# Side work of the tensor engine in pairs every second quarter, and the distance squares of one batch element dealt out anew

## The chip, the cores and the metric

The kernel runs on one core of one Trainium2 chip. The metric is the device time of one execution in microseconds (us), the median of several. TensorE (PE in the rows; PEld is its loading of weights), VectorE (DVE), ScalarE (ACT), GpSimd (POOL) and SyncE (SP, which issues the DMAs) each run their own list of instructions in order, and wait for each other through semaphores.

## What is computed

The input x is 8 x 1024 x 256 (batch elements, tokens, channels), fp32. Four residual blocks follow one another, each on a layer norm of x:

```python
x = x + attn_a(_layernorm(x))   # scores from distances between 3-d positions of the tokens, causal
x = x + ffn(_layernorm(x))      # mixes a token with the one before it; gate * (relu(k)**2 @ W_v)
x = x + attn_b(_layernorm(x))   # 16 heads of 16 channels, softmax over keys, causal
x = x + ffn(_layernorm(x))

# attn_a, the part that the change touches
pos = x @ w3d.T + b3d
sq = jnp.sum((pos[:, :, None, :] - pos[:, None, :, :]) ** 2, axis=-1)
dist = jnp.sqrt(sq)
attn = softmax(-dist * scale, causal)      # one matrix for all heads
out = (attn @ V) @ wo.T + bo
```

## The kernel before

**Two kinds of work.** The third block (attn_b, "att3" in the code) is the steady beat of the kernel. Its work is cut into PIECES = 8 elements x 4 groups of 4 heads x 12 pieces, and each piece into 4 **quarters**, one a head. Quarter u issues on PE one matmul for the row maxima (L922, into max_bank), one for the transposed scores (L935, into exp_bank, for a piece LEAD = 14 pieces earlier), and where u % 4 == 3 also the four products with the values (L954, into o_bank). DVE takes the maxima (L989, L992), ACT the exponentials (L973). max_bank and exp_bank have two buffers each. An element takes 192 quarters; call that a **turn**. Batch element n's third block runs in turn n.

Everything else (layer norms, first block "att1", the two FFNs "ffn2" and "ffn4", the projections of the third block "proj3") is **side work**. It is done for later elements while the beat runs. On PE it consists of **jobs** (`tr` transposes L442, `keys` L741, `receptance` and `products` L755, `project` L825, `values3` L841, `values1` L615, `positions` L600, `attend` L633, and `output` and `maxima` of the beat itself, L1066 and L1032). A job owns one of three PSUM banks (`side0` to `side2`) from its first part until ACT or DVE has read it (for `project` that is ACT's L784, for `tr` L432, for `positions` L519).

**The order.** `place()` runs before anything is issued: it goes quarter by quarter, from BEGIN = -224, and gives each part of each job its quarter and each job its bank. At most one part a quarter, no part before its due time; a job starts only if a bank is free by the plan. `shift` is how late the plan is. `schedule()` then writes each engine's instructions: in a quarter first those of att3, then those of the side work. The other engines' side instructions stand at the quarters `at(k)`, which are the stage's own times plus that shift.

**The prologue** is u < 0: no beat yet, only side work for elements 0 and 1. It ends when PE issues the first L922 at u = 0. Element 0's chain is: set up weights, att1, ffn2, proj3, store the projected parts to DRAM and load them as stacks, then u = 0. Element 1's att1 and ffn2 lie between.

**Squares of distances** (functions `dve_squares`, `act_att1`, `pool_att1`, `dve_att1`). Each of att1's 12 pieces (512, 384, 256, 128, then 512 five times, 384, 256, 128 columns) needs three squares, one a coordinate. ACT makes the first two (L536), POOL adds them (L589), DVE adds the third (L468, which also keeps it above a tiny value), and ACT transforms the sum in three steps: logarithm (L550), exp of half of it (L553), exp (L560). POOL cuts the diagonal (L578). The third square is made on DVE for elements 0 and 1 (L508 and L511, `n < 2`), on ACT for the others. In `act_att1` the instructions alternate: square of piece p, transform of piece p - 1, square, transform, transform. sq holds two pieces.

**Rows of ones.** The stacks of keys need two rows of ones, 2 partitions x 4096 elements in each of three stacks. They are set by DVE in `dve_weights` (L1151), at quarters that fall into element 0's att1.

Of the kernel before, what the change touches and what calls it, by code (L numbers as in the profile page):

```python
# [35 lines left out]
KROWS = HD * len(K_SLOTS)  # L36
SROWS = KROWS + 2
MAX_BANKS, EXP_BANKS = 2, 2
STACKS = 3
# [105 lines left out]
def place():  # L145

    parts, delay = [], {}
    for start, s, n, h in STAGES:
        for key, first, count, step, after in stage_jobs(s, n, h):
            delay[key] = after  # L150
            parts += [(start + first + step * k, key, k, k == count - 1) for k in range(count)]
    parts.sort(key=lambda part: part[0])
    rows = [(4 * NP * (g + 1) + 1, ("maxima", g)) for g in range(GROUPS)]
    rows += [(OUTPUT_AT[h] + 4 * NP * g + 5, ("output", g, h)) for g in range(GROUPS) for h in range(2)]
    rows += [(at, ("setup", k)) for k, at in enumerate(SETUP_AT)]
    rows.sort()
    quarters, bank, emptied, late = {}, {}, {}, []
    free, before, shift, u = [BEGIN, BEGIN, BEGIN], BEGIN, 0, BEGIN
    while parts or rows:
        while rows and rows[0][0] <= u and min(free) <= u:  # L160
            key = rows.pop(0)[1]
            k = free.index(min(free))
            quarters[key], bank[key], emptied[key] = [u], k, u + 2
            free[k] = u + 2
        if parts:
            at, key, k, last = parts[0]
            regained = max(0, shift - max(0, at - before) // 4)
            if at + regained <= u and (k > 0 or min(free) <= u):
                parts.pop(0)
                before, shift = at, max(regained, u - at)  # L170
                late.append((at, shift))
                if k == 0:
                    bank[key] = free.index(min(free))
                    free[bank[key]] = NEVER
                    quarters[key] = []
                quarters[key].append(u)
                if last:
                    emptied[key] = free[bank[key]] = u + delay[key]
        u += 1
    return quarters, bank, emptied, late  # L180

# [21 lines left out]
def bass_hybrid(nc, x, wq, bq, wk, bk, wv, bv, wo, bo, w3d, b3d, wkqv, bkqv, w_r, w_k, w_v,  # L203
# [7 lines left out]
    with ExitStack() as ctx:  # L211
# [310 lines left out]
        def act_att1(at, n):  # L522
# [37 lines left out]
                    act.activation(p1[:, at:at + w], d, ACT.Exp, scale=-SCALE).then_inc(p1_exp, 1)  # L560

            for p in range(NP + 1):
                for k in range(3):
                    if p < NP and (k < 2 or n > 1):
                        yield at(PIECE_AT[p] + PIECE_TIME[p] * 2 * k // 6)
                        square(p, k)
                    if p > 0:
                        yield at(PIECE_AT[p] + PIECE_TIME[p] * (2 * k + 1) // 6)
                        transform(p - 1, k)
# [565 lines left out]
        def dve_weights():  # L1135
# [10 lines left out]
            yield SETUP_AT[7] + 6  # L1146
            dve.tensor_copy(wv3[:, :, :, :], raw_kqv[:, :, :, 2 * HD:3 * HD])
            dve.memset(rinv1[:, :], 0.0).then_inc(weights_ready, 1)
            for r in range(STACKS):
                yield SETUP_AT[7] + 12 + 8 * r  # L1150
                dve.memset(ks[r][KROWS:SROWS, :, :], 1.0).then_inc(rows_of_ones, 1)  # L1151

        def pe_setup():
            pe = nc.tensor

# [44 lines left out]
        def pool_setup():  # L1200
            pool = nc.gpsimd
            yield SETUP_AT[6] + 6
            pool.memset(vp[:, :, ONE:ONE + 1], 1.0).then_inc(consts_ready, 1)
            for k, v in enumerate(v3):
                yield SETUP_AT[7] + 4 * k
# [84 lines left out]
        def _(dve):  # L1290
# [1 line left out]
            dve.wait_ge(consts_ready, 5)  # L1292

            def stage(at, s, n, h):
                body = {"att1": [dve_att1(at, n)] + ([dve_squares(at, n)] if n < 2 else []), "proj3": [dve_proj3(at, n), dve_values3(at, n)]}.get(s, []) if h == 0 else []
                return [dve_statistics(at, s, n, h)] + ([dve_ffn(at, s, n, h)] if s in ("ffn2", "ffn4") else body)

            schedule([dve_setup(), dve_weights()], dve_att3, dve_maxima, dve_output, stage)
# [36 lines left out]
```

## Time and profile before

| | |
|---|---|
| median of 3 runs | 2104.41 us (2093.51 to 2106.41) |
| the profiled execution, device time | 2109.85 us |
| its span, first to last instruction | 2108.1 us |
| busy: PE, DVE, ACT, POOL | 1849.2, 1467.0, 1323.7, 728.2 us |
| the prologue (to the first L922) | 195.1 us |
| a turn in the middle of the kernel | 245.8 us |
| after the last exponentials | 42 us |

The profiled execution is 5.4 us above the median of the three runs. "Busy" of PE counts a matmul until its modelled end, so it says where PE is fed without a gap, and not how much of its peak it reaches.

### The profile page before, as it was taken

The page shows a single profiled execution, that of the slowest core. Times are in us where ns is not written, and L with a number is a line of the kernel's source. Part 1 is how long each engine was busy: PE and PEld are TensorE (multiplying, and loading weights), DVE is VectorE, ACT ScalarE, POOL GpSimd, SP SyncE. Part 2 cuts the span into 40 slices and gives each one's busy share as a digit, 9 for nine tenths or more (in the row PEclk, how much of TensorE's full clock was granted, in tenths as well). Part 3 has the DMA queues.
Part 4 walks back from the last instruction along what each step waited for, and adds up shares of the span by engine and source line. Part 5 has one row for each costly group of instructions (what it writes and reads, how often), then busy time and mean ns, then how long its engine had stood idle before and what let it go on. Part 6 is the DMA issues. An engine that isn't in the chain of part 4 may idle for free. (4 is left out here: it accounts for less than half of the span.)

```text
span 2108.1 us, 32379 instructions
## 1 busy us (share of the span) xinstructions
PE 1849.2 (88%) x9842; PEld 922.5 (44%) x9842; DVE 1467.0 (70%) x4288; ACT 1323.7 (63%) x2585; POOL 728.2 (35%) x879
## 2 busy tenths in 40 slices
PE   5677898889997999889998899979998899988986
PEld 4453443335543455434543355434544345322423
DVE  5576778767676677667786667766776677768642
ACT  3564355876569565776758665695657766455664
POOL 1342332234333253333443243333532334312313
PEclk8797899999998999999999899989999999989998
DMA  3006113111131112410132111311124101322000
GB/s 85 1 23 123 26 56 67 31 31 32 55 76 31 31 31 82 80 21 12 41 110 42 31 31 56 76 31 31 34 83 76 22 11 41 99 33 50 13 21 20
DMA packets 64346, 97.26 MB, mean 46 GB/s; under 512 B 15655, under 2 KB 58029, under 8 KB 58030
## 3 DMA queue, kind: packets, MB, share of 16 engines
q1 hardware_dynamic: 64174, 95.20, 20.2%
q8 instruction: 80, 1.31, 0.3%
q14 instruction: 92, 0.75, 0.1%
HBM read 61.09 MB, written 33.55 MB: 45 GB/s over the span
## 5 line engine op out<-in xcount | busy, mean ns | idle before, releaser
L973 ACT ACTIVATE pt<-exp_bank 128x512 f32<-128x512 f32 (+1 forms) x1216 | 698.9, 582 | 526.6 <-PE exp_bank L935 521.0
L989 DVE CUSTOM_DVE_ANT_0 max_bank<-max_bank,mask 128x128 f32<-128x128 f32 (+3 forms) x1024 | 501.8, 500 | 400.9 <-PE max_bank L922 386.4
L922 PE MATMUL max_bank<-ks,qs 96*128 96x512 bf16 (+3 forms) x1536 | 523.5, 346 | 85.9 <-DVE piece_max L992 44.9
L935 PE MATMUL exp_bank<-qs,ks 98*128 98x512 bf16 (+3 forms) x1536 | 515.4, 342 | 40.0 <-ACT pt L973 37.0
L992 DVE TENSOR_REDUCE piece_max<-max_bank 128x1 f32<-128x512 f32 x512 | 344.1, 686 | 94.4 <-PE max_bank L922 90.2
L954 PE MATMUL o_bank<-pt,v 128*17 128x512 f32 (+3 forms) x3072 | 334.1, 508 | 13.7 <-POOL pt L1011 11.0
L922 PEld LDWEIGHTS max_bank<-ks,qs 96*128 96x128 bf16 x1536 | 150.9, 99 | 399.5 <-DVE piece_max L989 140.9
L1011 POOL TENSOR_SCALAR_AFFINE_SELECT pt<-pt 128x512 f32<-128x512 f32 x256 | 171.5, 670 | 412.6 <-ACT pt L973 411.8
L935 PEld LDWEIGHTS exp_bank<-qs,ks 98*128 98x128 bf16 x1536 | 152.4, 100 | 236.0 <-ACT pt L973 118.5
L633 PE MATMUL side<-vp,p 128*128 128x260 f32 x576 | 171.4, 423 | 28.7 <-ACT p L560 21.0
L412 ACT ACTIVATE xh<-xs,shift,rstd 128x256 f32<-128x256 f32 x256 | 149.7, 596 | 47.8 <-POOL shift L401 47.8
L589 POOL TENSOR_TENSOR sq<-sq 128x512 f32<-128x512 f32 (+1 forms) x96 | 97.3, 1013 | 226.3 <-ACT sq L536 226.3
L536 ACT ACTIVATE sq<-pb,neg_pos 128x512 f32<-128x512 f32 (+3 forms) x264 | 167.0, 633 | 3.6 <-ACT p L560 0.4
L741 PE MATMUL side<-pb,wkT 128*128 128x512 f32 x240 | 139.3, 669 | 9.3 <-DVE pb L675 9.2
L989 DVE DVE_READ_ACCUMULATOR2_ANT piece_max<- 128x1 f32 x1024 | 144.5, 141 | 0.3
L633 PEld LDWEIGHTS side<-vp,p 128*128 128x128 f32 x576 | 111.2, 207 | 74.1 <-issue 31.1
L825 PE MATMUL side<-xt,wkq 128*128 128x512 f32 x256 | 136.8, 619 | 3.0 <-ACT xt L432 1.5
L755 PE MATMUL side<-wrT,pb 128*128 128x256 f32 x480 | 126.3, 387 | 0.0
L755 PE MATMUL side<-wvT,pb 128*128 128x256 f32 x480 | 125.7, 386 | 0.0
L1090 POOL TENSOR_TENSOR xs<-xs,on 128x256 f32<-128x256 f32 x64 | 49.3, 770 | 208.5 <-DVE on L1080 208.4
L664 POOL TENSOR_TENSOR xs<-xs,tm 128x512 f32<-128x512 f32 x64 | 98.3, 1541 | 66.2 <-DVE tm L692 66.2
L791 POOL TENSOR_TENSOR parts<-x,parts 128x512 bf16<-128x512 f32 x64 | 74.9, 1170 | 108.3 <-DVE parts L775 108.3
(119 smaller groups left out, 2348.4 us busy)
## 6 DMA issues: line engine op xcount, KB each, us to landing
parts_dram<-parts SPq DMA_DIRECT2D x64, 384.0 KB, 2.6
qs<-parts_dram SPq DMA_DIRECT2D x192, 128.0 KB, 7.2
ks<-parts_dram SPq DMA_DIRECT2D x32, 384.0 KB, 4.7
xs<-in_L_attn_a_x_dram SPq DMA_DIRECT2D x16, 512.0 KB, 4.2
ks<-parts_dram SPq DMA_DIRECT2D x32, 256.0 KB, 5.4
out_dram<-xs SPq DMA_DIRECT2D x16, 512.0 KB, 3.1
ks<-parts_dram SPq DMA_DIRECT2D x32, 128.0 KB, 5.8
qs<-neg_maxT SPq DMA_DIRECT2D x64, 8.0 KB, 1.9
```

The costliest lines, as they stand in the source:

```text
L412: act.activation(xh[:, t, :], src[:, TPH * h + t, :], ACT.Identity, bias=shift[:, r, t:t + 1], scale=rstd[:, r, t:t + 1]).then_inc(xh_read ...
L536: mm = act.activation(sq[:, p % 2, c, 0:w], pb[:, c, q0:q1], ACT.Square, bias=neg_pos[:, kt, c:c + 1])
L633: mm = pe.matmul(bank[:, 0:VC], p1[:, at:at + P], vp[:, kt, :], start=(kt == 0), stop=(kt == t))
L741: mm = pe.matmul(bank[:, :], wkT[:, c, P * j:P * (j + 1)], xk[:, c, :], start=(c == 0), stop=(c == NC - 1))
L755: mm = pe.matmul(bank[:, C * t:C * (t + 1)], lhs[:, c, P * (2 * j + t):P * (2 * j + t + 1)], rhs[:, c, :], start=(c == 0), stop=(c == NC - 1))
L922: pe.matmul(max_bank[u % MAX_BANKS][:, 0:k1 - k0], qs[r][0:KROWS, j, P * tile:P * (tile + 1)], ks[r][0:KROWS, j, k0:k1], start=True, stop= ...
L935: mm = pe.matmul(exp_bank[k % EXP_BANKS][:, (q1 - q0) * slot:(q1 - q0) * (slot + 1)], ks[r][:, j, P * kt:P * (kt + 1)], qs[r][:, j, q0:q1] ...
L954: mm = pe.matmul(o_bank[32 * j:32 * j + VW, q0 - HALF * h:q1 - HALF * h], v3[n % 2][:, kt, GH * (g % NG) + j, :], pt[:, (e - 1) % 2, j, 0: ...
L973: act.activation(pt[:, e % 2, j + 1 - heads:j + 1, 0:w], exp_bank[k % EXP_BANKS][:, 0:heads * w].rearrange("p (j n) -> p j n", j=heads), A ...
L989: dve.tensor_tensor_reduce(scores, scores, mask[:, HALF - w:HALF], 1.0, LOWEST, ALU.add, ALU.max, piece_max[:, j, m:m + 1]).then_inc(max_f ...
L992: dve.tensor_reduce(piece_max[:, j, m:m + 1], scores, AX.X, ALU.max).then_inc(max_free, 1)
L1011: pool.affine_select(out=block, in_=block, compare_op=ALU.is_ge, fill=0.0, base=0, pattern=[[0, GH], [1, P]], channel_multiplier=-1).then_ ...
```

## The change

1. `place()`: for u < 0 it is as before, one part a quarter. For u >= 0 parts are placed in odd quarters only, up to two of them, and a part may be taken one quarter ahead of its due time (first part of a job) or two quarters ahead (a later part). Bank rules stay.
2. `act_att1`, element 0: the two squares of piece p stand together ahead of the three transforms of piece p - 1.
3. `dve_squares` is used for element 0 alone; for element 1 the third square goes to ACT, as it did for elements 2 to 7.
4. The three settings of rows of ones go from `dve_weights` to `pool_setup`, ahead of POOL's other settings there, behind a wait for the second layer norm's shift.

```diff
-        if parts:
+
+        for _ in range(1 if u < 0 else 2 * (u % 2)):
+            if not parts:
+                break
             at, key, k, last = parts[0]
             regained = max(0, shift - max(0, at - before) // 4)
-            if at + regained <= u and (k > 0 or min(free) <= u):
-                parts.pop(0)
...
+            if at + regained > u + (u >= 0) * (1 if k == 0 else 2) or k == 0 and min(free) > u:
+                break
+            parts.pop(0)
...
             for p in range(NP + 1):
+                for k in range(2 if n == 0 and p < NP else 0):
+                    yield at(PIECE_AT[p] + k)
+                    square(p, k)
                 for k in range(3):
-                    if p < NP and (k < 2 or n > 1):
+                    if p < NP and n > 0:
                         yield at(PIECE_AT[p] + PIECE_TIME[p] * 2 * k // 6)
                         square(p, k)
...
-            for r in range(STACKS):
-                yield SETUP_AT[7] + 12 + 8 * r
-                dve.memset(ks[r][KROWS:SROWS, :, :], 1.0).then_inc(rows_of_ones, 1)
...
             yield SETUP_AT[6] + 6
+            pool.wait_ge(shift_ready, 2)
+            for r in range(STACKS):
+                pool.memset(ks[r][KROWS:SROWS, :, :], 1.0).then_inc(rows_of_ones, 1)
+            pool.wait_ge(rows_of_ones, STACKS)
             pool.memset(vp[:, :, ONE:ONE + 1], 1.0).then_inc(consts_ready, 1)
...
-                body = {"att1": [dve_att1(at, n)] + ([dve_squares(at, n)] if n < 2 else []), ...
+                body = {"att1": [dve_att1(at, n)] + ([dve_squares(at, n)] if n == 0 else []), ...
```

Lines of the changed kernel stand 4 lower from `place()` to `act_att1`'s loop and 7 lower behind it: L536 is L540, L550 is L554, L468 is L472, L922 is L929, L935 is L942, L954 is L961, L825 is L832, L841 is L848.

**Place 1, element 0's att1, DVE.** From the last settings of the transposed weights to the end of the second piece (384 columns). Before:

```order
L1133 COPY wvT<-side 128x256 x2
L1151 MEMSET ks 2x4096
L508 TENSOR_SCALAR sq<-pb,neg_pos 128x512
L511 TENSOR_TENSOR sq<-sq 128x512
L468 SCALAR_TENSOR_TENSOR sq<-sq 128x512
L508 TENSOR_SCALAR sq<-pb,neg_pos 128x384
L511 TENSOR_TENSOR sq<-sq 128x384
L1151 MEMSET ks 2x4096
L468 SCALAR_TENSOR_TENSOR sq<-sq 128x384
```

Now:

```order
L1140 COPY wvT<-side 128x256 x2
L512 TENSOR_SCALAR sq<-pb,neg_pos 128x512
L515 TENSOR_TENSOR sq<-sq 128x512
L472 SCALAR_TENSOR_TENSOR sq<-sq 128x512
L512 TENSOR_SCALAR sq<-pb,neg_pos 128x384
L515 TENSOR_TENSOR sq<-sq 128x384
L472 SCALAR_TENSOR_TENSOR sq<-sq 128x384
```

The settings of `ks` have left DVE's list; a third one stood in the same way ahead of the 128-column piece. On ACT in the same place, squares of the 384- and 256-column pieces and transforms of the pieces before them. Before:

```order
L536 ACTIVATE sq<-pb,neg_pos 128x384
L550 ACTIVATE sq<-sq 128x512
L536 ACTIVATE sq<-pb,neg_pos 128x384
L553 ACTIVATE sq<-sq 128x512
L560 ACTIVATE p<-sq 128x512
L536 ACTIVATE sq<-pb,neg_pos 128x256
L550 ACTIVATE sq<-sq 128x384
```

Now:

```order
L540 ACTIVATE sq<-pb,neg_pos 128x384 x2
L554 ACTIVATE sq<-sq 128x512
L557 ACTIVATE sq<-sq 128x512
L564 ACTIVATE p<-sq 128x512
L540 ACTIVATE sq<-pb,neg_pos 128x256 x2
L554 ACTIVATE sq<-sq 128x384
```

The second square of a piece no longer stands behind the logarithm of the piece before it.

**Place 2, element 1's att1, ACT**, among the steps of element 0's FFN gate (L713, L717, L720 before; L720, L724, L727 now). Before:

```order
L560 ACTIVATE p<-sq 128x512
L536 ACTIVATE sq<-pb,neg_pos 128x256
L550 ACTIVATE sq<-sq 128x384
L713 ACTIVATE xs<-side 128x512
L720 ACTIVATE xs<-xs 128x512
L536 ACTIVATE sq<-pb,neg_pos 128x256
L717 ACTIVATE xs<-xs 128x512
L553 ACTIVATE sq<-sq 128x384
L560 ACTIVATE p<-sq 128x384
L720 ACTIVATE xs<-xs 128x512
```

Now:

```order
L564 ACTIVATE p<-sq 128x512
L540 ACTIVATE sq<-pb,neg_pos 128x256
L554 ACTIVATE sq<-sq 128x384
L720 ACTIVATE xs<-side 128x512
L727 ACTIVATE xs<-xs 128x512
L540 ACTIVATE sq<-pb,neg_pos 128x256
L724 ACTIVATE xs<-xs 128x512
L557 ACTIVATE sq<-sq 128x384
L540 ACTIVATE sq<-pb,neg_pos 128x256
L564 ACTIVATE p<-sq 128x384
L727 ACTIVATE xs<-xs 128x512
```

One more square a piece stands ahead of the gate's last step.

**Place 3, the projections of a later element, PE, with buffer numbers.** Project job 2 of element 5 and the first part of job 3. Before:

```order
L825 MATMUL side1<-xt,wkq 128x512
L922 MATMUL max_bank1<-ks1,qs1 128x128
L935 MATMUL exp_bank0<-qs2,ks2 128x256
L954 MATMUL o_bank<-pt,v30 17x384 x4
L825 MATMUL side1<-xt,wkq 128x512
L922 MATMUL max_bank0<-ks1,qs1 128x256
L935 MATMUL exp_bank1<-qs2,ks2 128x128
L841 MATMUL side0<-wv3,xt 128x256 x2
L922 MATMUL max_bank1<-ks1,qs1 128x256
L935 MATMUL exp_bank1<-qs2,ks2 128x128
L825 MATMUL side2<-xt,wkq 128x512
```

Now:

```order
L832 MATMUL side2<-xt,wkq 128x512 x2
L929 MATMUL max_bank0<-ks1,qs1 128x128
L942 MATMUL exp_bank0<-qs2,ks2 128x256
L929 MATMUL max_bank1<-ks1,qs1 128x128
L942 MATMUL exp_bank0<-qs2,ks2 128x256
L961 MATMUL o_bank<-pt,v30 17x384 x4
L832 MATMUL side2<-xt,wkq 128x512
```

Job 2's two parts stand together, and job 3 follows in the same bank two quarters later, where before it had another bank. The plan's shift at the middle turns is 0 to 2 quarters, where before it was 0 to 4.

## Rows read from the trace of the kernel before

**Rows 1.** Stretches A:B: length; busy PE, PEld, DVE, ACT, POOL (count); granted clock, DMA, GB/s
```profile
0.00:195.10 195.10, 128.23 (x514) 94.58 (x514) 121.31 (x278) 105.86 (x205) 68.53 (x91) 0.85 0.19 46
394.70:633.50 238.80, 218.05 (x1228) 110.95 (x1224) 176.22 (x528) 162.79 (x325) 90.28 (x108) 1.00 0.22 50
...
1370.80:1616.60 245.80, 225.89 (x1228) 113.95 (x1224) 176.54 (x526) 164.91 (x328) 91.03 (x108) 0.96 0.21 48
```

**Rows 2.** The same for stretches of turn 4, and where its clock falls
```profile
1125.10:1180.20 55.10, 43.86 (x238) 17.01 (x235) 36.70 (x108) 49.31 (x102) 19.46 (x27) 0.91 0.18 30
...
1207.00:1338.50 131.50, 127.90 (x664) 67.49 (x663) 98.49 (x289) 80.62 (x154) 55.93 (x60) 0.97 0.17 47
...
1207.10:1213.80 6.70, 6.09 (x19) 1.74 (x18) 5.94 (x11) 3.74 (x7) 1.82 (x3) 0.50 0.00 0
```

**Rows 3.** DVE in order of time: start, length, line, instruction [idle before <-what ended it]
```profile
40.59 0.69 DVE L468 SCALAR_TENSOR_TENSOR sq<-sq 128x512 f32<-128x512 f32 x1
...
43.12 3.47 DVE L1151 MEMSET ks<- 2x4096 bf16 x1 [0.91 <-DVE sq L511]
46.62 0.56 DVE L468 SCALAR_TENSOR_TENSOR sq<-sq 128x384 f32<-128x384 f32 x1
...
54.94 0.28 DVE L468 SCALAR_TENSOR_TENSOR sq<-sq 128x128 f32<-128x128 f32 x1
```

**Rows 4.** POOL in order of time, the same stretch
```profile
23.15 0.55 POOL L1206 MEMSET v<- 128x128 f32 x2
37.73 1.26 POOL L589 TENSOR_TENSOR sq<-sq 128x512 f32<-128x512 f32 x1 [14.03 <-ACT sq L536]
42.53 1.00 POOL L589 TENSOR_TENSOR sq<-sq 128x384 f32<-128x384 f32 x1 [3.54 <-ACT sq L536]
...
50.30 0.46 POOL L589 TENSOR_TENSOR sq<-sq 128x128 f32<-128x128 f32 x1 [0.73 <-ACT sq L536]
```

**Rows 5.** POOL's settings of other tiles, from one line's view: durations in ns min/median/max
```profile
L1262 POOL MEMSET ident<- x1: 205/205/205, 0.8 to 0.8; 128x128 f32 x1
L1262 POOL MEMSET mask<- x1: 530/530/530, 1.1 to 1.1; 128x512 f32 x1
```

**Rows 6.** ACT in order of time: pieces of element 0, then the gate of its FFN
```profile
58.35 0.63 ACT L550 ACTIVATE sq<-sq 128x512 f32<-128x512 f32 x1 [0.79 <-DVE sq L468]
...
63.04 0.63 ACT L550 ACTIVATE sq<-sq 128x512 f32<-128x512 f32 x1 [1.42 <-DVE sq L468]
...
136.18 0.61 ACT L720 ACTIVATE xs<-xs 128x512 f32<-128x512 f32 x1
```

**Rows 7.** PE in order of time, prologue
```profile
57.88 3.80 PE L633 MATMUL side<-vp,p 128*128 128x260 f32 x8 [3.86 <-issue]
...
80.59 2.04 PE L741 MATMUL side<-pt,wkT 128*128 128x512 f32 x2 [7.27 <-issue]
```

**Rows 8.** Stretches of 20 us, element 1's att1 beside element 0's proj3
```profile
120.00:140.00 20.00, 19.64 (x88) 14.17 (x87) 11.47 (x25) 16.18 (x36) 8.08 (x11) 1.00 0.01 1
140.00:160.00 20.00, 10.86 (x38) 6.65 (x36) 19.56 (x38) 9.61 (x19) 10.44 (x10) 0.90 0.17 59
```

**Rows 9.** Groups: line, count | busy us, mean ns | idle (L536: 100 to 200 us)
```profile
L536 ACT ACTIVATE sq<-pb,neg_pos 128x512 f32<-128x512 f32 (+3 forms) x24 | 14.6, 608 | 0.8
L511 DVE TENSOR_TENSOR sq<-sq 128x512 f32<-128x512 f32 (+3 forms) x24 | 15.0, 623 | 0.8
L508 DVE TENSOR_SCALAR sq<-pb,neg_pos 128x512 f32<-128x512 f32 (+3 forms) x24 | 12.7, 528 | 0.1
```

**Rows 10.** Turn 4, PE and ACT in order of time: banks' matmuls, a reader, waits
```profile
1303.81 1.13 PE L841 MATMUL side<-wv,xt 128*128 128x256 f32 x4 [0.82 <-ACT xt L432]
...
1307.37 1.02 PE L825 MATMUL side<-xt,wkq 128*128 128x512 f32 x2
...
1309.15 0.68 ACT L784 ACTIVATE x<-side,cols 128x512 f32<-128x512 f32 x1
...
1335.59 0.63 PE L442 MATMUL side<-ident,xh 128*128 128x128 f32 x4 [0.59 <-ACT x L784]
```

More of the change, by code:

```diff
@@ L164, in place @@
             free[k] = u + 2
-        if parts:
+        for _ in range(1 if u < 0 else 2 * (u % 2)):
+            if not parts:
+                break
             at, key, k, last = parts[0]
             regained = max(0, shift - max(0, at - before) // 4)
-            if at + regained <= u and (k > 0 or min(free) <= u):
-                parts.pop(0)
[L170 to L178, printed above, removed]
+            if at + regained > u + (u >= 0) * (1 if k == 0 else 2) or k == 0 and min(free) > u:
+                break
+            parts.pop(0)
+            before, shift = at, max(regained, u - at)
+            late.append((at, shift))
+            if k == 0:
+                bank[key] = free.index(min(free))
+                free[bank[key]] = NEVER
+                quarters[key] = []
+            quarters[key].append(u)
+            if last:
+                emptied[key] = free[bank[key]] = u + delay[key]
         u += 1
@@ L1294, in stage @@
             def stage(at, s, n, h):
-                body = {"att1": [dve_att1(at, n)] + ([dve_squares(at, n)] if n < 2 else []), "proj3": [dve_proj3(at, n), dve_values3(at, n)]}.get(s, []) if h == 0 else []
+                body = {"att1": [dve_att1(at, n)] + ([dve_squares(at, n)] if n == 0 else []), "proj3": [dve_proj3(at, n), dve_values3(at, n)]}.get(s, []) if h == 0 else []
                 return [dve_statistics(at, s, n, h)] + ([dve_ffn(at, s, n, h)] if s in ("ffn2", "ffn4") else body)
```

## Prediction, made before the changed kernel ran

> **What bounds the kernel now.** I read the busy times of the page first (the table above): PE is busy for 88% of the span, DVE 70%, ACT 63%. A share over the whole span hides the stages, so the second view is that of stretches. It shows three parts. The prologue takes 195.1 us, with no engine busy for more than two thirds of it: a chain of waits. A turn takes 245.8 us in the middle of the kernel and 238.8 us once, early, with the same 1228 PE matmuls; the granted clock is 1.00 in the short one and 0.96 in the long ones [rows 1]. Third, within a turn the first 55 us have ACT busy for 49.3 (it bounds them), and the 131 us from the FFNs to the projections have PE busy for 127.9 [rows 2]. Where ACT bounds, it is idle for nothing a PE order could mend; where PE bounds, only 3.6 us a turn are PE idle time.
>
> So edit 1 (pairs) works in the turns, and edits 2 to 4 work in the prologue, where the plan's quarters are unchanged. Whatever the prologue loses, the end loses: the beat starts when element 0's stacks are loaded.
>
> **Edit 4, rows of ones off DVE.** Each takes 3.47 us on DVE [rows 3]. What counts is how late each makes the sum of the piece it stands ahead of. First piece: POOL's sum of two squares ends at 37.73 + 1.26 = 38.99 [rows 4], DVE adds the third at 40.59 [rows 3]: 1.6 us late. Second: 43.53 against 46.62, 3.1 us. Fourth: 50.76 against 54.94, 4.2 us, of which I leave 1.2 for four short instructions of DVE's own that stand between: 3.0. ACT's logarithm waits for each. Sum 7.7 us.
>
> On POOL, no setting of 4096 elements stands in the trace. 128 elements take 205 ns and 512 take 530 [rows 5], a slope of 0.85 ns an element: 3.6 us each, 10.7 for the three. They start when POOL is free of the second layer norm, 23.1, end near 34, and the small settings behind them [rows 4] near 34.6. POOL's next work is the sum at 37.73, idle for 14 us before it. So they cost nothing, with 3 us to spare; bounds are nothing and, at twice the slope, 21 us, which ends at 45 and makes the first sum 7 us late. I take the slope: it is the same operation on the same engine. The GPSIMD Engine Reference of the Trainium skill (introduction) calls GpSimd the wrong choice for ordinary elementwise arithmetic, the Vector engine being "roughly 2x faster". By that rule the settings would end at 45 and the saving would nearly be used up; DVE's 3.47 us for 4096 are 0.85 ns an element too, so for settings this trace does not agree with it.
>
> **Edit 2, squares ahead.** With a square between logarithm and transform, one 512-column piece follows the other in 63.04 - 58.35 = 4.7 us [rows 6]: logarithm, square, POOL's sum, DVE's sum, one behind the other. With both squares ahead, POOL and DVE work while ACT transforms the piece before, and ACT's own five instructions set the pace: 2 x 0.7 + 3 x 0.63 + 0.3 for their hand-overs = 3.6 us. But layer norm 2 of the first half waits for the first four pieces only (the attend job of PE at 57.88 [rows 7]), and there it gives some 0.5 us. The five later long pieces gain 1.1 us each; PE comes to their attends only behind the first keys job at 80.59 [rows 7], which waits for that layer norm and not for them. I take 0.5, with 0 and 6 as bounds. Edits 2 and 4: -8.
>
> **Edit 3, element 1's third square from DVE to ACT.** It takes half of 27.7 us, 13.9, from DVE and adds 12 x 0.61 = 7.3 us to ACT [rows 9]. From 120 to 140 us ACT is the fuller of the two (16.2 of 20, DVE 11.5) [rows 8]; four added squares (0.7 + 0.6 + 0.5 + 0.4 = 2.2 us) stand ahead of the gate's last step, which ends at 136.8 [rows 6], and through it POOL's sum into x and the layer norm of proj3: +2.2. From 140 to 160 DVE is full (19.6 of 20) [rows 8] and that layer norm's statistics stand in its queue behind the squares of three pieces, 3 x 1.15 = 3.5 us: -3.5. Later squares are in ACT's gaps or the like on both sides. Net -1; bounds -4 (ACT's gaps take all) and +7 (all of ACT's share is late).
>
> **Edit 1, pairs.** No matmul is added. Half of the odd quarters hold the value products, and half the pairs follow them; before, a quarter of the parts did, so the switches are as many. With two buffers for maxima and for scores, two quarters' beat (0.9 us) then two parts (1.7 us) leave DVE and ACT the same 2.6 us to give a buffer back. What moves are the waits for side banks and inputs. A reader takes its time: project's last matmul ends at 1308.39, the bank is free at 1309.83, 1.4 us [rows 10]. Now job 3 follows job 2 in one bank with 0.85 us of PE work between (place 3): 0.7 us of waiting. In the same way, counted from the order at 1.4 to 1.7 us a reader: job 1 0.4, the output job behind project 7 0.9, the third positions job 1.0, and the two first values jobs, now two quarters behind their transposes instead of three, 0.9 each. Sum 4.9 us a turn. What goes are such waits of before: 0.82 and 0.59 [rows 10], and six smaller of the kind and the first attend's in the same turn, 4.4 in all by my reading of PE's order of time. Net +0.5 a turn, +3 for the six full turns; bounds -2.5 and +4 a turn.
>
> **Sum.** -8 - 1 + 3 = -6 us on the profiled execution's 2109.85: 2103.9. That execution is 5.4 above the median of the runs shown, so on the median's scale 2098.
>
> **Rivals.**
> - *The turns lose their clock falls.* At 1207.10 the clock is at half (1.2 of 2.4 GHz) for 6.7 us, just as the FFNs begin [rows 2]; the turn without falls is 7.0 us shorter [rows 1]. The keys jobs now start a quarter earlier and closer together, so a fall could pass. For it: the same work did run a turn at 1.00. Against: PE's load in the stretch before does not change, and four turns repeat the fall. All four: 28 us less, 2070 on the median's scale.
> - *Side banks bind more than I count* (the other side: slower). Place: projections to positions, where DVE and PE are both near full, so a reader's 1.4 us is often longer. If all new waits come and none of the old goes: +4.9 x 6 = 29 instead of 3, 2124. It decides from 1.5 us a turn on, where it eats the prologue's 9. The clock may join in, from 1.00 to 0.5 in places. The page TensorE: Matmul & The Clock Gate of the Trainium skill ("A second HAM failure mode") says that small idle times between groups of matmuls make the clock oscillate, which speaks against pairs with bare quarters between; rows here show falls in the thin stretches alone.
> - *POOL at twice the slope:* +7, 2105.
> - *The prologue gives nothing:* element 1's squares on ACT are late by their full 7.3 instead of -1. -8 + 7 + 3: 2106 and, without edit 1's 3, 2103.
>
> **Chances.** Forecast 0.46, clock falls lost 0.18, banks bind 0.16, POOL 0.05, prologue for nothing 0.15. One per cent, about what a measurement of this kernel can tell from no change, is 21 us: below 2083 or above 2125. The first rival lies mostly below, with a tail of the forecast: faster 0.25. The second is over 2125 in its worst part, and with a clock fall more: slower 0.11. Range: 2072 takes in half of the first rival, 2120 the second up to 4 us a turn (2098 + 3.5 x 6 = 2119).
>
> **What would show it.** The first L922 starts near 186 instead of 195.1; element 0's attend job for the fourth tile starts near 50 instead of 57.88; POOL's settings end before 35. In element 1, statistics of proj3's second half end some 1 to 3 us earlier than the shift of the whole. Turns of 246 +/- 3 with falls at the same place say that pairs are neutral; turns near 239 at 1.00 are the first rival; idle time of PE ahead of side jobs over 8 us a turn is the second. Settings of 7 us on POOL are the third. If the prologue shrinks by 9 and the end does not, a turn has taken it back, and the view by turns says which.

## The result and the profile after

| | before | changed |
|---|---|---|
| median | 2105.41 us | 2214.32 us (2211.22 to 2225.35, 4 runs) |
| ratio, 95% interval | | 1.054 (1.0487 to 1.0594) |
| profiled execution, device time / span | 2109.85 / 2108.1 us | 2211.22 / 2209.5 us |
| first beat (u = 0) | 195.1 us | 193.2 us |
| turns 1 to 5, mean length | 244.4 us | 262.4 us |
| of that, without PE busy | 20.2 us | 34.8 us |

The changed kernel is 5.4% slower. The forecast was 2098 us and the range ended at 2120. A fourth execution of the kernel before took 2414.66 us; it moves that median from 2104.41 to 2105.41 us, and the ratio is that of fast executions alone.

The first view of the changed kernel is that of stretches, one a turn from u = 192 on (columns as in [rows 1]):

```profile
397.40:656.50 259.10, 223.85 (x1229) 111.95 (x1225) 171.97 (x525) 162.81 (x326) 87.78 (x108) 0.98 0.21 46
656.50:921.40 264.90, 230.90 (x1227) 115.20 (x1225) 172.86 (x527) 164.21 (x328) 88.19 (x108) 0.95 0.20 45
921.40:1182.60 261.20, 225.37 (x1229) 112.78 (x1225) 172.93 (x527) 163.87 (x328) 88.52 (x108) 0.97 0.21 45
```

The first of them answers to the turn of 238.8 us in [rows 1]. The matmuls are as many (1229) and the clock is nearly as high (0.98). Yet it takes 20 us more, and 14.5 us of these are PE idle time: 259.10 - 223.85 = 35.3 against 20.8. Over turns 1 to 5 the mean grows by 18.0 us, 14.6 of them idle, 3.4 busy at a lower clock. Five such turns are 90 us; turn 0, turn 6 and the tail add 4.5, 6.7 and 2.0, and the prologue takes 1.9 off. That is the 101.4 us between the two spans. Within a turn, 13.2 of the 18.0 us lie in quarters 73 to 166, the stretch in which PE was busy nearly all the time [rows 2]: 143.3 us in place of 130.1 on average, with 14.8 us of PE idle time in place of 3.3.

The second view is that of PE's waits over the whole run: what PE was about to do, whom it waited for, us in total, times, longest. Before:

```profile
PE max_bank L922 <- DVE piece_max L992: 44.9, 80, 1.4
PE side L442 <- ACT xh L412: 22.8, 7, 9.7
PE side L741 <- DVE pb L675: 9.2, 3, 3.6
```

and changed:

```profile
PE side L446 <- ACT xh L416: 61.5, 45, 9.7
PE max_bank L929 <- DVE piece_max L999: 47.4, 78, 1.7
PE side L748 <- DVE pb L682: 40.6, 29, 3.6
PE side L1039 <- DVE neg_max L1008: 13.7, 21, 1.0
PE side L622 <- ACT xt L436: 10.6, 8, 1.8
PE side L832 <- ACT x L791: 6.7, 7, 1.1
```

The two waits that grew most, by 70 us together, are not for a bank. They are for *inputs* of side jobs: xh, the normalised rows that `tr` transposes, and the mixed rows (in pb) that `keys` multiplies. Of the waits for xh some 21 us belong to the prologue in either kernel. From the first beat on they are, before and changed:

```profile
PE side L442 <- ACT xh L412: 1.8, 3, 1.3
PE side L446 <- ACT xh L416: 41.5, 41, 1.6
```

All of PE's waits from the first beat on, added up: ahead of side jobs 48.7 us before and 138.4 changed, ahead of the beat's own matmuls 133.7 and 136.8. So the idle time came almost wholly ahead of side jobs. Waits for the reader that gives a side bank back, the rival I had priced, went from 13 to 29 us (L832 <- L791 is 6.7 of them); xh and the mixed rows went from 11 to 82.

One such wait, turn 4, PE in order of time:

```profile
1254.43 0.38 PE L929 MATMUL max_bank<-ks,qs 96*128 96x512 bf16 x1
1254.65 0.33 PE L942 MATMUL exp_bank<-qs,ks 98*128 98x384 bf16 x1
1255.72 0.66 PE L446 MATMUL side<-ident,xh 128*128 128x128 f32 x4 [0.74 <-ACT xh L416]
```

and ACT beside it:

```profile
1254.69 0.49 ACT L980 ACTIVATE pt<-exp_bank 128x384 f32<-128x384 f32 x1 [1.06 <-PE exp_bank L942]
1255.08 0.59 ACT L416 ACTIVATE xh<-xs,shift,rstd 128x256 f32<-128x256 f32 x1
```

This xh stands in ACT's order in quarter 60, behind that quarter's place in the beat. PE issues the beats of quarters 60 and 61 within 0.4 us, because quarter 60 has no part any more, and stands before the transpose of quarter 61 while ACT has just come to the exponential ahead of the xh. So ACT waits for PE (1.06 us), and then PE for ACT (0.74 us). Before, the same transpose stood in quarter 62:

```profile
1195.55 1.04 PE L633 MATMUL side<-vp,p 128*128 128x260 f32 x4
...
1197.19 0.60 PE L442 MATMUL side<-ident,xh 128*128 128x128 f32 x4
```

A part of 1.04 us lay between the beats of quarters 60 and 61 (L922 at 1195.16 and 1196.42), then came the beat of quarter 62, and the xh was there.

### The profile page after: what moved, and what is told of

Same layout as the page of the kernel before. It is cut to its first block and busy times, and to the rows that moved or that the text cites. A ratio compares the mean times of both kernels' runs of the same rounds, so it can differ in the third digit from the quotient of the medians.

```text
span 2209.5 us, 32354 instructions
## 1 busy us (share of the span) xinstructions
PE 1862.3 (84%) x9842; PEld 924.9 (42%) x9842; DVE 1433.9 (65%) x4261; ACT 1320.0 (60%) x2597; POOL 722.1 (33%) x882
## 5 line engine op out<-in xcount | busy, mean ns | idle before, releaser
L980 ACT ACTIVATE pt<-exp_bank 128x512 f32<-128x512 f32 (+1 forms) x1216 | 685.8, 579 | 591.1 <-PE exp_bank L942 588.8
L996 DVE CUSTOM_DVE_ANT_0 max_bank<-max_bank,mask 128x128 f32<-128x128 f32 (+3 forms) x1024 | 495.4, 503 | 459.9 <-PE max_bank L929 449.4
L929 PE MATMUL max_bank<-ks,qs 96*128 96x512 bf16 (+3 forms) x1536 | 513.7, 343 | 89.1 <-DVE piece_max L999 47.4
L942 PE MATMUL exp_bank<-qs,ks 98*128 98x512 bf16 (+3 forms) x1536 | 502.6, 338 | 39.3 <-ACT pt L980 36.6
L961 PE MATMUL o_bank<-pt,v 128*17 128x512 f32 (+3 forms) x3072 | 338.1, 513 | 14.6 <-POOL pt L1018 11.8
L929 PEld LDWEIGHTS max_bank<-ks,qs 96*128 96x128 bf16 x1536 | 151.7, 99 | 375.3 <-DVE piece_max L996 134.4
L942 PEld LDWEIGHTS exp_bank<-qs,ks 98*128 98x128 bf16 x1536 | 152.1, 100 | 189.8 <-ACT pt L980 89.8
L540 ACT ACTIVATE sq<-pb,neg_pos 128x512 f32<-128x512 f32 (+3 forms) x276 | 171.6, 626 | 3.6 <-ACT p L564 0.4
L640 PE MATMUL side<-vp,p 128*128 128x260 f32 x576 | 157.0, 409 | 15.3 <-ACT p L564 10.4
L748 PE MATMUL side<-pb,wkT 128*128 128x512 f32 x240 | 130.4, 671 | 40.6 <-DVE pb L682 40.6
L446 PE MATMUL side<-ident,xh 128*128 128x128 f32 x512 | 84.1, 291 | 69.6 <-ACT xh L416 61.5
L832 PE MATMUL side<-xt,wkq 128*128 128x512 f32 x256 | 134.8, 626 | 8.9 <-ACT x L791 6.7
L762 PE MATMUL side<-wrT,pb 128*128 128x256 f32 x480 | 116.6, 386 | 0.0
L762 PE MATMUL side<-wvT,pb 128*128 128x256 f32 x480 | 116.6, 386 | 0.0
L446 PEld LDWEIGHTS side<-ident,xh 128*128 128x128 f32 x512 | 58.1, 145 | 135.2 <-ACT xh L416 89.2
```

What stands on the lines that cost most here:

```text
L540: mm = act.activation(sq[:, p % 2, c, 0:w], pb[:, c, q0:q1], ACT.Square, bias=neg_pos[:, kt, c:c + 1])
L640: mm = pe.matmul(bank[:, 0:VC], p1[:, at:at + P], vp[:, kt, :], start=(kt == 0), stop=(kt == t))
L748: mm = pe.matmul(bank[:, :], wkT[:, c, P * j:P * (j + 1)], xk[:, c, :], start=(c == 0), stop=(c == NC - 1))
L762: mm = pe.matmul(bank[:, C * t:C * (t + 1)], lhs[:, c, P * (2 * j + t):P * (2 * j + t + 1)], rhs[:, c, :], start=(c == 0), stop=(c == NC - 1))
L929: pe.matmul(max_bank[u % MAX_BANKS][:, 0:k1 - k0], qs[r][0:KROWS, j, P * tile:P * (tile + 1)], ks[r][0:KROWS, j, k0:k1], start=True, stop= ...
L942: mm = pe.matmul(exp_bank[k % EXP_BANKS][:, (q1 - q0) * slot:(q1 - q0) * (slot + 1)], ks[r][:, j, P * kt:P * (kt + 1)], qs[r][:, j, q0:q1] ...
```

## The experiments

Two theories stood at the start. **Inputs late**: a part that is moved ahead meets an input whose producer stayed at its place, behind its own quarter's beat. **Bunched**: two parts in one go hold back the beat. Neither is the whole. The differences in us below are the measured ratio less 1, times about 2100.

### Which edit

> The kernel before with edit 1 alone: the rule that places the side jobs' parts, nothing else. All theories that put the loss into the side parts expect nearly the whole difference: the turns of the changed kernel are 14 to 20 us longer each, its prologue is 1.9 us shorter, so 2211 to 2220 us here. A theory that the memsets on POOL or the third squares on ACT cost the time expects 2105 us.

2219.37 us, ratio 1.0578 (1.0527 to 1.0630). Edit 1 carries the whole loss: 121 us beside 114, with intervals that overlap.

> Edits 2, 3 and 4 without edit 1: the changed kernel with the old rule for the side jobs' parts. If edit 1 carries the whole loss, this gains what the prologue shows in the changed kernel's trace, 1.9 us, and about 1 us at element 1: 2100 to 2104 us. DVE's copies between 24 and 33.4 us should again take 2.2 to 3.6 us in place of 0.43, beside POOL's memsets.

2102.91 us, ratio 1.0004 (0.9971 to 1.0037). No difference can be measured. First beat at 194.2 us, so most of the 9 us that the prediction gave to the prologue are missing, and the loss in the turns is another matter. A first beat is read from one execution and has a spread of its own: in the eight kernels whose instructions up to it are those of the kernel before, it lies between 194.4 and 198.4 us, 196.7 on average. With edits 2 to 4 as in the changed kernel it lies at 191.8, 193.2 and 194.2.

### Pairs and lead apart

Pairs, nothing earlier:

```diff
 PARTS_AT, BANK, EMPTIED_AT, LATE = place()      # as before
+MOVED = ("setup", "maxima", "output")
+PARTS_AT = {key: [u + (u >= 0 and u % 2 == 0 and key[0] not in MOVED) for u in at] for key, at in PARTS_AT.items()}
```

> Pairs without looking ahead: the side jobs are planned as before, and then every part of an even quarter moves into the odd one behind it. 2 parts stand between two beats of the attention as in the changed kernel, but no part stands earlier than before. Theory 'inputs late' (TensorE stands before parts whose input comes from engines that are still behind their quarter's beat): no input is needed earlier, so about 2105 us, at most 2115. Theory 'bunched' (two parts together hold back the beat, whose rings of banks then run dry): about the same loss as the changed kernel, 2190 us or more.

2132.15 us, ratio 1.0168 (1.0118 to 1.0217): +35 us.

Lead, no pairs:

```diff
-        for _ in range(1 if u < 0 else 2 * (u % 2)):
+        for _ in range(1):
```

> Looking ahead without pairs: at most one part in a quarter, in every quarter, but by the changed rule a part may stand 1 (a job's first) or 2 quarters ahead of its time. The parts stand on average 1.17 quarters earlier than before, in the changed kernel 1.18. Theory 'inputs late': the same margin of 1 quarter, 2.2 us, is taken from every input, so a loss like the changed kernel's, 2170 to 2215 us. Theory 'bunched': about 2105 us.

2138.03 us, ratio 1.0193 (1.0133 to 1.0253): +41 us.

Both theories missed both numbers. Each half costs something, and 35 + 41 = 76 falls short of the 114 to 121 us of the two together. The waits say that the two costs are of different kinds. Pairs without lead:

```profile
PE max_bank L924 <- DVE piece_max L994: 64.5, 97, 1.4
PE side L444 <- ACT xh L414: 22.8, 7, 9.7
PE o_bank L956 <- POOL pt L1013: 21.0, 23, 1.5
PE side L743 <- DVE pb L677: 9.2, 3, 3.6
```

Lead without pairs:

```profile
PE max_bank L926 <- DVE piece_max L996: 41.1, 74, 2.0
PE side L745 <- DVE pb L679: 31.9, 30, 3.6
PE side L446 <- ACT xh L416: 29.9, 14, 9.7
PE o_bank L958 <- POOL pt L1015: 3.8, 9, 1.2
```

Pairs leave the inputs as before (22.8 and 9.2) and lengthen the waits of the beat itself (maxima from 44.9 to 64.5). Lead leaves the beat and lengthens the waits for inputs (9.2 to 31.9, 22.8 to 29.9). The sums from the first beat on, in us:

| kernel | PE's waits ahead of side jobs | ahead of the beat |
|---|---|---|
| before | 48.7 | 133.7 |
| pairs in odd quarters | 37.8 | 164.4 |
| lead, single parts | 85.9 | 117.9 |
| changed | 138.4 | 136.8 |

In the changed kernel the price that pairs have alone, waits of the beat, has gone again, and all the loss stands ahead of side jobs.

The run with lead and single parts changes one thing more. The side instructions of the other engines are written by the plan's shift, and a plan with lead is less late. Worked out from the plans, they stand one or two quarters earlier in 30% of the quarters there and in 22% in the changed kernel, 0.35 and 0.34 quarters on average; in the runs that move parts after the plan is made they stand where they stood. No run has the lead of this one with those instructions held in place, so its 41 us are not shown to be those of the parts alone. The next run is free of this.

### How much lead

```diff
-            if at + regained > u + (u >= 0) * (1 if k == 0 else 2) or k == 0 and min(free) > u:
+            if at + regained > u + (u >= 0) * 1 or k == 0 and min(free) > u:
```

> The kernel before with pairs, but the lead cut to 1 quarter for every part: 415 of 844 parts of the attention's quarters stand 1 quarter earlier than before, 429 where they stood (in the changed kernel 375 stand 1, 249 stand 2 and 40 stand 3 quarters earlier). If the cost of a pair grows with the lead, this lies between the pairs without lead (+34 us) and the changed kernel (+115 us): by the mean leads (-0.5, 0.49 and 1.18 quarters) at +80 us, 2180 us. If only parts that stand 2 or more quarters early reach their inputs too soon, it lies near the pairs without lead: 2130 to 2145 us.

2161.78 us, ratio 1.0272 (1.0250 to 1.0293): +57 us. It lies between the two forecasts, so the loss begins with the first quarter of lead and grows behind it. Here the other engines' side instructions stand as in the kernel before. Against the pairs without lead, the same 415 parts stand two quarters earlier, and the readers of their banks with them: 22 us more, and the waits ahead of side jobs go from 37.8 to 87.5 us.

### The inputs earlier

> The changed kernel with the inputs that TensorE waited for most moved 2 quarters ahead in their engines' orders: the layer norms (statistics on DVE, deviation on POOL, xh on ACT) and the token mixing of the feed-forward (xk and xr on DVE). Everything else as in the changed kernel. Theory 'inputs late': the waits of the changed kernel for xh (61.5 us in all, 22.8 before) and for the mixing (40.6 us, 9.2 before) fall back to about the old values, so 60 to 70 us are regained: about 2145 us, with the waits for other inputs and for the maxima left. Theory 'bunched' (pairs themselves, whatever stands in them): nothing is regained, 2200 us or more.

2182.60 us, ratio 1.0367 (1.0338 to 1.0396). About 35 us come back, not 60 to 70. The named waits went as forecast: xh is at its old value, and mixing is down from 40.6 to 6.4, 74 us less together. But in the profiled execution the beat's own waits grew by 26 us, from 136.8 to 162.5, and PE was busy for 21 us more at a lower clock (0.939 beside 0.948):

```profile
PE max_bank L936 <- DVE piece_max L1006: 62.0, 103, 1.7
PE exp_bank L949 <- ACT pt L987: 41.8, 92, 1.3
PE side L452 <- ACT xh L422: 21.3, 5, 10.0
```

> The changed kernel with every clocked instruction of ACT, DVE, POOL and SP that belongs to side work moved 1 quarter ahead (the takers of the side banks stay where they are). The parts stand 1.18 quarters ahead on average, so this gives back most of the lead to the inputs, but not to the second parts of pairs, which stand 2 ahead. Theory 'inputs late': more than half of the 115 us regained, 2120 to 2155 us, not less than the 2132 us of the kernel with pairs and no lead by more than 10. Theory 'bunched': 2200 us or more.

2175.55 us, ratio 1.0345 (1.0305 to 1.0385): 40 us come back, less than "more than half".

> Pairs with a lead of at most 1 quarter (+55 us when run before), and every clocked instruction of side work on ACT, DVE, POOL and SP 1 quarter ahead. Against their inputs the parts stand on average 0.51 quarters later than before, like the pairs without lead (0.49). Theory 'the lead costs by the inputs, the pair by the beat': the two are the same, +34 us within 10: 2125 to 2145 us, with waits for xh near 22 us. If the side work that is now ahead of the beats on ACT and DVE costs in its own right: +50 us or more.

2152.06 us, ratio 1.0269 (1.0222 to 1.0316). The same as without the earlier inputs (1.0272), where 1.016 was forecast. xh fell from 38.1 to 22.6 us, as said, and the wait for POOL's part of the beat rose from 11.6 to 28.0. The next run shows that price alone.

> The kernel with the rows of ones set on ACT and edits 2 and 3, and in addition every clocked instruction of side work on ACT, DVE, POOL and SP 1 quarter ahead in its engine's order, with the parts of TensorE where they always stood. If the old places of the inputs already left TensorE waiting (37 us of waits for side inputs in the kernel before lie mostly in the prologue), up to 5 us are gained on the 2081 to 2094 us of the kernel without it; if the beats of DVE and ACT are now held back by work that is not yet due, the waits for the maxima grow and it is slower by 5 to 15 us. Forecast: within 1% of the kernel without it.

2136.27 us, ratio 1.0183 (1.0128 to 1.0238), where the kernel without it has 0.9928 (below): 2.6% slower, 54 us. The forecast of "within 1%" is wrong. To have the inputs earlier has a price of its own:

```profile
PE max_bank L925 <- DVE piece_max L995: 50.7, 83, 1.4
PE exp_bank L938 <- ACT pt L976: 43.7, 93, 1.0
PE o_bank L957 <- POOL pt L1014: 29.2, 34, 1.6
PE side L442 <- ACT xh L412: 22.5, 6, 10.1
```

Waits for POOL's part of the beat, 11.4 us in the kernel without it, are 29.2 here, and those for the exponentials rose from 35.9 to 43.7; all waits of the beat together from 131.6 to 162.6. Each move by one quarter also changes which side instruction stands behind which instruction of the beat on three engines. That this is the reason is argued, not shown. So the runs that moved inputs measure a gain less this price and can't size "inputs late" alone; that it exists is shown by the waits, not by their times. In the changed kernel itself, where side instructions moved too, the beat's waits hardly grew (133.7 to 136.8), so nothing like this price shows there.

### Which quarter

In the even quarters instead, nothing earlier (`u % 2 == 1` in the diff of the pairs without lead):

> Pairs without looking ahead as in the run with +34 us, but in the even quarters: every part of an odd quarter moves into the even one behind it. The value products of the attention (4 matmuls, every fourth quarter, always an odd one) then no longer stand beside a pair. Theory 'pairs hold back the beat': +25 to +45 us again. Theory 'the pair collides with the value products': at most +10 us, 2098 to 2116 us.

2090.88 us, ratio 0.9976 (0.9946 to 1.0006). The same pairs cost nothing. "Bunched" falls, in the form in which I had put it. It is the place of the pair.

> Pairs without lead, but only in every fourth quarter, that of the value products: parts of quarters with remainder 2 by 4 move into the one with remainder 3, all others stay. Theory 'collision with the value products': these 227 moved parts carry nearly the whole loss of the pairs in odd quarters, +25 to +35 us, 2125 to 2135 us. Theory 'odd quarters as such (the exponentials run there)': half of it, +17 us, 2115 us.

2133.89 us, ratio 1.0135 (1.0090 to 1.0179): +28 us.

> The counterpart: parts of quarters with remainder 0 by 4 move into the one with remainder 1, behind which no value products stand. Theory 'collision': within 8 us of the kernel before, 2090 to 2106 us. Theory 'odd quarters as such': +17 us, 2115 us.

2115.40 us, ratio 1.0058 (1.0034 to 1.0082): +12 us. So 28 of the 35 to 40 us belong to the quarter with the value products (227 parts moved), 12 to the other odd one (188 parts moved). The forecasts were 25 to 35, and under 8 or 17. The mean time from one quarter's L922 to the next, in us, worked out from the starts of all of them in turns 1 to 6, shows what happens there:

| kernel | u % 4 = 0 | 1 | 2 | 3 | four quarters |
|---|---|---|---|---|---|
| before | 0.88 | 1.07 | 1.17 | 1.94 | 5.06 |
| pairs in odd quarters | 0.43 | 1.56 | 0.62 | 2.55 | 5.16 |
| pairs in even quarters | 1.40 | 0.58 | 1.67 | 1.37 | 5.02 |
| lead, single parts | 0.86 | 1.23 | 1.20 | 1.84 | 5.13 |
| changed | 0.38 | 2.00 | 0.58 | 2.45 | 5.41 |
| changed, pairs in even | 1.53 | 0.60 | 1.72 | 1.30 | 5.15 |

The quarter of the value products is the longest already. A pair there, without lead, makes it 2.55 us on average, and in turn 4's quarter 91 of that kernel it is 3.3 us from L922 to L922 (1248.59 to 1251.87). DVE and ACT have two quarters of beat in their buffers for that time and no more; then the next two beats follow within 0.4 us of each other, and PE waits for DVE. In the even quarters the long stretches of PE work are 1.4, 1.7 and 1.4 us.

> The changed kernel with its pairs in the even quarters, all else as in it. The planner then gives the parts a mean lead of 0.66 quarters in place of 1.18 (6 parts 3 quarters ahead, 111 two, 368 one, 304 none, 55 one behind). Theory 'an odd quarter is the wrong place for a pair, since every second one carries the value products': the 34 us of the pairs go, and what the lead costs beside single parts (40 us at a lead of 1.17) goes down with it, so 2105 to 2130 us. Theory 'pair and lead together cost, wherever the pair stands': by the lead alone (+55 us at 0.49, +115 us at 1.18) 2160 us or more.

2142.24 us, ratio 1.0175 (1.0125 to 1.0225): +37 us in place of +114. The place takes two thirds of the loss away, with the lead going from 1.18 to 0.66 quarters as part of it. It is 12 us above the forecast's upper end of 2130. Its waits of the beat add up to 137.2 us, as in the changed kernel; those ahead of side jobs fell from 138.4 to 81.4. So in the changed kernel the odd quarters, and the larger lead that goes with them, cost through the inputs and not through the beat. The waits:

```profile
PE max_bank L929 <- DVE piece_max L996: 52.0, 128, 1.3
PE max_bank L929 <- DVE piece_max L999: 47.5, 78, 1.8
PE side L446 <- ACT xh L416: 24.0, 8, 10.1
```

Why pair and lead together cost more than their sum is to be seen by the transposes. Of the 55 `tr` pairs of the beat's time (one for each half layer norm), so many have their first part one quarter behind the last xh, the others two or more:

| kernel | one behind | what stands in the quarter between the two | waits for xh |
|---|---|---|---|
| before | 0 | a part | 22.8 us, 7 times |
| pairs in odd, no lead | 0 | | 22.8 us, 7 times |
| lead, single parts | 43 | a part, mostly | 29.9 us, 14 times |
| pairs in odd, lead of 1 | 40 | nothing | 38.1 us, 39 times |
| changed | 46 | nothing | 61.5 us, 45 times |
| changed, pairs in even | 9 | | 24.0 us, 8 times |

(The counts are worked out from the plan, the waits read from the traces; some 21 us and 4 times of each are the prologue's.) The last xh mostly stands in an even quarter. With single parts that quarter still has its part, which gives ACT its time. With pairs in odd quarters it is bare, 0.4 us long, and PE arrives at once. The waits for xh and mixing together are 61.5 + 40.6 us in the changed kernel and 29.9 + 31.9 in the one with single parts and lead, 40 us more, beside the 38 us by which 114 exceeds 76. That fits, but it isn't proof: where the waits were taken away by earlier inputs, 74 us of them, only 35 came back. Why the changed kernel waits 23 us longer for xh than the pairs with a lead of 1, at nearly the same count, stays open.

### The prologue

Here the changed kernel's DVE, in order of time, from 24 us on:

```profile
24.00 2.23 DVE L1151 COPY wkq<-p 128x128 f32<-128x128 f32 x2
26.16 0.74 DVE L456 TENSOR_TENSOR vp<-side,bias_vp 128x259 f32<-128x259 f32 x2
26.82 3.01 DVE L1151 COPY wkq<-p 128x128 f32<-128x128 f32 x2
29.76 3.56 DVE L463 TENSOR_SCALAR neg_pos<-vp 128x12 f32<-128x12 f32 x1
29.82 3.49 DVE L1140 COPY wrT<-side 128x256 f32<-128x256 f32 x1
30.16 3.29 DVE L1151 COPY wkq<-p 128x128 f32<-128x128 f32 x2
```

and POOL's settings:

```profile
22.58 10.71 POOL L1208 MEMSET ks<- 2x4096 bf16 x3
```

Three settings, 3.57 us each on average, end near 26.1, 29.7 and 33.3. DVE's copies, 0.44 us for two of them before, end at 26.23, 29.83 and 33.45. A tensor_scalar on 12 elements a partition took 3.56 us, 0.17 before. Each was held until the setting beside it was over, and PE then waited, by its waits:

```profile
PE side L622 <- DVE wrT L1140: 4.2, 1, 4.2
```

The positions jobs began at 39.22 us in place of 31.75, 7.5 us later, and that is all that was to be saved (7.7).

> The kernel before with edits 2 and 3, and the three memsets of the rows of ones neither on DVE nor on POOL but on ACT, which has nothing to do from 2.1 to 13.0 us of the span. Theory 'POOL's memset holds DVE': with the memsets away from POOL DVE's copies between 24 and 34 us take 0.43 us again, the first element's pieces start 7 to 8 us earlier than before, and the prediction's gain of the prologue comes true in part: the first beat of the attention at 186 to 190 us in place of 195.1, the whole 4 to 8 us shorter than before, 2090 to 2094 us. Theory 'the prologue is bound elsewhere' (a load, the order of TensorE's parts): the pieces start early, the first beat stays within 2 us of 195.1, and no difference can be measured.

```diff
+            act.wait_ge(consts_ready, 5)
+            half = minus_half[KROWS:SROWS, 0:1].unsqueeze(2).to_broadcast([SROWS - KROWS, GH, S])
+            for r in range(STACKS):
+                act.activation(ks[r][KROWS:SROWS, :, :], half, ACT.Copy, scale=-2.0).then_inc(rows_of_ones, 1)
```

2094.28 us, ratio 0.9928 (0.9903 to 0.9954). The first kernel whose interval leaves out 1 on the fast side: 15 us by the ratio, 12 by the medians. First beat at 185.0 us. Its rows:

```profile
2.75 10.62 ACT L1289 ACTIVATE ks<-minus_half 2x4096 bf16<-2x4096 f32 x3 [0.67 <-POOL xt L1270]
...
28.36 0.44 DVE L1147 COPY wkq<-p 128x128 f32<-128x128 f32 x2
```

The same copies take 0.44 us again. Against the kernel with edits 2 to 4 alone, where they took as long as in the changed one, only the engine of the settings differs. So it was POOL's settings that held them.

> The kernel before with the three memsets of the rows of ones on ACT from 2.8 us of the span on, and no other edit. By the prediction's terms (7.7 us for the memsets, 0.5 us for the squares ahead, 1 us for the third squares of element 1 on ACT) this keeps 7.7 of the 8 to 10 us which the kernel with edits 2 and 3 had at its first beat: first beat at 186 to 188 us. If the squares' place is worth more than that forecast, it lies at 190 us or later.

2089.26 us, ratio 0.9966 (0.9939 to 0.9994). First beat at 188.5 us, 6.6 before that of the kernel before and 8.2 before the average of 196.7 given above: around the 7.7 of the sum. From 188.5 to 185.0 there are 3.5 us more for edits 2 and 3, forecast at 0.5 and 1. But the last kernel below, with the same prologue as the one at 185.0, has its first beat at 187.2, so what they give is 1.3 to 3.5 us, inside the spread of such readings.

> The version that the runs point to: the kernel before with the rows of ones set on ACT, edits 2 and 3, and every part of an odd quarter moved into the even quarter behind it. If the two gains add (0.9928 and 0.9976 to 1), 0.990, about 2078 us; if the pairs in even quarters are worth nothing beside it, 0.993, 2084 us.

2086.29 us, ratio 0.9912 (0.9877 to 0.9947). Faster than the kernel before and the changed one, and not to be told apart from the one with the rows of ones alone (0.9928). The gain of the pairs in even quarters isn't shown.

## Why the prediction was wrong, point by point

- **What bounds the kernel.** The reading that PE bounds the dense stretch (127.9 of 131.5 us, [rows 2]) was right. What follows from it was not drawn: where PE has 3.6 us to spare a turn, a new wait in front of a part has next to nothing to hide in. That stretch took 13.2 of the 18.0 us that a turn gained in length.
- **Edit 1, the step that failed.** "What moves are the waits for side banks and inputs" was written, and then only the banks were added up: 4.9 us a turn for their readers, 4.4 taken off. Of the inputs only the transposed rows of the first values jobs were counted, 0.9 us twice; xh and the mixed rows were held at nothing, without a reason. What was missing is that a producer stands in its engine's order behind the beat of its quarter, and this beat is released by PE. A part that moves a quarter ahead takes the PE work of that quarter out from between. Measured: 70 us more of waits for these two inputs, where the term was 3 us in all. (The list of new waits adds up to 4.8 us, not 4.9, and its first entry is 1.4 - 0.85 = 0.55 by its own figures, not 0.7. Nothing hangs on either.)
- **"two quarters' beat (0.9 us) then two parts (1.7 us) leave DVE and ACT the same 2.6 us"** failed as well. It took an average quarter. Half of the pairs stand behind the value products, and that quarter goes from 1.94 to 2.55 us: 28 of the 35 us which pairs without lead cost. In the changed kernel this did not show as waits of the beat (136.8 us beside 133.7), but as bare quarters in which inputs are not ready: with the pairs in even quarters the waits for xh and the mixed rows are 67 us less. I had the value products in view and counted only how often the PE work switches, not how long it lasts.
- **Rival 2** had the side (slower) and the stretch (where PE is near full). Its mechanism, readers of banks, came in part: 16 us more of such waits where the sum had 3 and the worst case 29. But that is a small part of the loss, and the worst case, 2124, was 90 us short. The range therefore failed through a term that none of its bounds took in.
- **Rival 1** did not happen. The falls of the clock stayed: a mean of 0.94 to 0.98 in turns 1 to 5 against 0.96 to 1.00.
- **Edit 4, rows of ones on POOL.** The duration was right (3.57 us each, forecast 3.6; end 33.3, forecast 34) and so was POOL's idle time. "So they cost nothing" was wrong, since the cover was looked for on POOL alone and DVE's copies of that time were not asked. The saving on DVE was about right: 6.6 to 8.2 us at the first beat, where 7.7 was forecast, when the settings go to ACT. The SBUF — State Buffer page of the Trainium skill (section "Who interferes with whom") says it: a DVE copy or tensor_scalar between SBUF tiles can run in a mode that takes two pairs of ports, one of them shared with GpSimd, and "whoever issues first gets the shared pair for the whole instruction". The trace agrees (two copies of 0.44 us together took 2.2, 3.0 and 3.3). I had weighed another page, on GpSimd's speed, and this one not. What the hold took from the sum is all but the whole of edit 4: 191.8 to 194.2 us with the settings on POOL, 185.0 and 187.2 with them on ACT.
- **Edits 2 and 3.** Forecast 0.5 and 1 us. Measured together, 1.3 to 3.5 us at the first beat, within their bounds (0 to 6, and -4 to 7). In the changed kernel itself the attend job for the fourth tile, forecast near 50 us, started at 58.46: the signs named for the prologue had all failed but the end of POOL's settings.
- **Sum.** The terms outside edit 1 came to nothing (ratio 1.0004) where -9 was forecast, edit 1 to +114 to +121 where +3 was.

## What to carry to other kernels

Before an instruction is moved ahead on one in-order engine, list for each one what it waits for, and ask what releases the producer: if that is the moved engine itself, the work that you take out from between is the producer's time. When regular work is gathered into larger portions, put them where the period is short, not beside its longest step. And an idle engine is free for a job only if it shares nothing with the engines that are busy at that time. Place decided twice here: the same pairs cost nothing in even quarters, and the same settings gave some 7 us on ACT.

## What the runs showed of the hardware

- Setting 2 x 4096 bf16 elements took 3.47 us on DVE, 3.57 on POOL and 3.54 on ACT (10.62 for three). None of the three is quicker by more than 3%; what differs is who else is held.
- A setting on POOL (3.57 us) held DVE's copies (0.26 us each by themselves) and a tensor_scalar (0.17) between SBUF tiles until its end, however small they were. Two of DVE's additions of a PSUM and an SBUF tile, issued at 26.16 us beside the second setting, were over after 0.74 us.
- With both squares ahead of the transforms, DVE's third add of 512 columns took 1.47 us in place of 0.69 [rows 3] where it ran beside a sum of POOL. POOL and DVE in the kernel without edit 1, in order of time:

```profile
45.98 2.22 POOL L592 TENSOR_TENSOR sq<-sq 128x512 f32<-128x512 f32 x2 [11.40 <-ACT sq L536]
```

```profile
47.28 1.47 DVE L468 SCALAR_TENSOR_TENSOR sq<-sq 128x512 f32<-128x512 f32 x1 [3.05 <-POOL sq L592]
```
